# Attention over two buffers of exponentials, key scores inside the solve, diagonal blocks turned on chip

## The chip, the cores and the metric

One Trainium2 chip, of which the kernel uses one core. The metric is the device time of one execution in microseconds. Three runs of the kernel before took 1352.12, 1353.29 and 1354.02 us; the median is 1353.29.

## The reference

The kernel computes two layers: attention and a mixture of 64 experts, then a linear attention and a mixture of 8 experts, over two sequences of 512 tokens of width 256. Only the first attention is changed. Cut to what matters:

```python
# B = 2 sequences, T = 512, H = 16 heads of D = 16; q, k rotated (rope), scale = 1/4
s = einsum('bihd,bjhd->bhij', k, k) * scale        # keys against keys
e = exp(s - max over j < i), 0 where j >= i
p = e / sum(e)
A = eye(T) + p * beta[..., None]                   # unit lower triangular
u = solve_triangular(A, v, lower=True)
sc = einsum('bihd,bjhd->bhij', q, k) * scale, -inf where j > i
o = einsum('bhij,bhjd->bihd', softmax(sc), u)
x = x + o.reshape(B, T, 256) @ Wo
```

## The kernel before

The attention is worked in four units of eight heads of one sequence (UNITS = 4, GH = 8). In a unit the 512 rows are four blocks of 128 (NI = 4). The split bf16 parts of k and q lie in `stk`, three stacks (k, B, q) with two buffers each. TensorE, VectorE (dve), ScalarE (act), GpSimd (pool) and the DMA queue of SyncE (sp) each run one program written out by hand; semaphores order them. A unit passes these stages:

1. Row maxima. `row_scores` (L310) multiplies one head's scores into a bank pair `slot` of the PSUM tensor `scores`, and `maxima` (L571) reduces it on VectorE, one head and kind (key, query) at a time, sixteen rounds in all. `maxima` splits the eight heads' results in three bf16 parts, `turn_maxima` (L302) turns them, `rows` (L758) copies them to `mrow`, and SyncE puts them in the stacks as three more rows.
2. Key exponentials. `transposed_scores` (L323) gives one head's transposed scores less the maxima, `exps` (L764) its exponential in `E`, `select` (L847) on GpSimd clears the part above the diagonal. The sums over them are matmuls into `misc` (L355); their copy (L776), turn (L362) and `scale` (L592) give the factor `ng`, and turned again `G`.
3. Inversion. SyncE writes the diagonal blocks of `E` to DRAM (`edd`, L894) and reads their 32x32 blocks back turned, one per partition row, into `LB` (L900). `invert` (L615) multiplies by G (L624), runs 31 steps of products and sums (L638, L647) on VectorE, and copies the result turned (L651). SyncE writes both forms to DRAM (`xsd`) and reads them back into `XT` and `XR` (L910), which GpSimd has cleared.
4. Levels. In eight steps q the 32x32 inverses are joined to 64x64 (q below 4) and to 128x128: `sums` (L367) on TensorE, `scaled_sums` (L671) on VectorE, `join` (L387) on TensorE, `joined` (L654) on VectorE. Between the steps lie rounds of row maxima of the next unit: `maxima_due` (L244) gives which, all sixteen in unit 0 and the eight query ones in units 1 and 2.
5. Solve. `solve` (L411) with `solved` (L683): four steps, each a chain of matmul, bank copy on ScalarE (L809, L814), turn, and VectorE work, ending in a block of `U` (L697). In its last two steps four heads of the next unit's key scores are put in.
6. The next unit's key softmax (stage 2, the rest), then this unit's query exponentials, `attend` (L446) against U, `turn_outputs` and `outputs` (L701). The query exponentials lie in `EQ`, four heads deep, so that head 4 waits for the first half of `attend`.
7. For units 2 and 3, the eight key maxima ahead of the levels (`ahead`, L240), two slots at once.

VectorE's order in the loop over units is the spine of it:

```python
for q in range(8):
    if q: joined(u, q - 1)
    scaled_sums(u, q)
    for m in maxima_due(u + 1, q): maxima(u + 1, m, 0)
joined(u, 7); solved(u)
scale(u + 1); invert(u + 1)
outputs(u)
for m in range(ahead(u + 2)): maxima(u + 2, m, m % 2)
```

Ahead of the loop come the layer norm, the projections (`project`, L276) with rotation and split (`rotate_and_split`, L548), and stages 1 to 3 of unit 0.

## Time and profile before

| | |
|---|---|
| median of three runs | 1353.29 us |
| the profiled execution | 1339.94 us |
| its span | 1337.9 us |
| TensorE busy in the span | 823.5 us (62%) |
| VectorE | 569.6 us (43%) |
| ScalarE | 219.4 us (16%) |
| GpSimd | 250.8 us (19%) |
| granted TensorE clock, mean | 0.70 |

The profile is of one execution. Its span is 2.0 us shorter than that execution's own time. An instruction belongs to a line of the kernel; matmuls are pipelined and their ends are modelled. A clock of 1.00 is 2.4 GHz, one of 0.50 is 1.2 GHz.

### The profile page before, as it was taken

The page shows a single profiled execution, that of the slowest core. Times are in us where ns is not written, and L with a number is a line of the kernel's source. Part 1 is how long each engine was busy: PE and PEld are TensorE (multiplying, and loading weights), DVE is VectorE, ACT ScalarE, POOL GpSimd, SP SyncE. Part 2 cuts the span into 40 slices and gives each one's busy share as a digit, 9 for nine tenths or more (in the row PEclk, how much of TensorE's full clock was granted, in tenths as well). Part 3 has the DMA queues.
Part 4 walks back from the last instruction along what each step waited for, and adds up shares of the span by engine and source line. Part 5 has one row for each costly group of instructions (what it writes and reads, how often), then busy time and mean ns, then how long its engine had stood idle before and what let it go on. Part 6 is the DMA issues. An engine that isn't in the chain of part 4 may idle for free. (4 is left out here: it accounts for less than half of the span.)

```text
span 1337.9 us, 16296 instructions
## 1 busy us (share of the span) xinstructions
PE 823.5 (62%) x5790; PEld 538.4 (40%) x5791; DVE 569.6 (43%) x1712; ACT 219.4 (16%) x345; POOL 250.8 (19%) x303
## 2 busy tenths in 40 slices
PE   5376367675876687536740039999950455099990
PEld 3232145323632463134340028888840224056660
DVE  5265965158606850832154003333333655123332
ACT  1021000330033003300310013333310121021110
POOL 4010000230032003400106740000027710400004
PEclk9658655675567557655755569999975666599995
DMA  3605830088017602180049248887833300211113
GB/s 122 83 2 119 148 140 0 4 126 208 2 36 108 193 3 63 35 257 1 0 149 405 106 147 269 271 269 270 272 110 98 97 25 0 74 37 47 43 35 102
DMA packets 133774, 149.81 MB, mean 112 GB/s; under 512 B 57552, under 2 KB 96848, under 8 KB 132688
## 3 DMA queue, kind: packets, MB, share of 16 engines
q1 hardware_dynamic: 106032, 85.00, 22.8%
q10 hardware_dynamic: 20000, 43.00, 11.4%
q0 software_dynamic: 7680, 20.98, 4.9%
q8 instruction: 39, 0.64, 0.2%
q14 instruction: 23, 0.19, 0.0%
HBM read 81.89 MB, written 66.85 MB: 111 GB/s over the span
## 5 line engine op out<-in xcount | busy, mean ns | idle before, releaser
L576 DVE TENSOR_REDUCE nm<-scores 128x1 f32<-128x128 f32 (+3 forms) x256 | 106.3, 483 | 45.5 <-PE scores L319 45.0
L1023 PE MATMUL scores<-xgT,wgu 128*96 128x256 f32 x512 | 121.6, 380 | 0.0
L1092 DVE TENSOR_TENSOR hT<-sg,scores 96x256 f32<-96x256 f32 x64 | 26.7, 417 | 194.1 <-ACT sg L1129 194.1
L1213 POOL DMA_INDIRECT gb<-expert_outputs,gather_slots x64 | 66.9, 1045 | 223.6 <-SPq L1206 204.4
L854 POOL TENSOR_SCALAR_AFFINE_SELECT E<-E 128x256 f32<-128x256 f32 x64 | 24.5, 406 | 430.0 <-ACT E L769 430.0
L1000 PE MATMUL misc<-cf,xg 128*128 128x128 f32 x256 | 39.3, 277 | 93.6 <-DMA xg<-expert_rows 93.6
L1023 PEld LDWEIGHTS scores<-xgT,wgu 128*96 128x96 f32 x512 | 80.4, 164 | 20.8 <-issue 0.3
L1452 PE MATMUL scores<-w,xgT 128*128 x184 | 87.9, 601 | 0.3 <-issue 0.3
L316 PE MATMUL scores<-stack_B,stack_k 96*128 96x128 bf16 (+3 forms) x128 | 49.9, 468 | 53.1 <-DVE nm L576 25.0
L319 PE MATMUL scores<-cb 128*128 128x128 bf16 x256 | 80.0, 314 | 0.0
L1140 POOL DMA_INDIRECT expert_rows<-xn_moe,scatter_slots x64 | 62.5, 977 | 70.0 <-DVE gather_slots L1069 50.8
L1000 PEld LDWEIGHTS misc<-cf,xg 128*128 128x128 f32 x256 | 32.7, 143 | 100.1 <-issue 93.7
L1008 PE MATMUL scores<-wd,hT 96*128 96x256 f32 x256 | 65.9, 379 | 0.1
L1121 ACT COPY xgT<-misc 128x512 f32<-128x512 f32 x64 | 37.5, 586 | 158.5 <-PE misc L1000 158.5
L316 PE MATMUL scores<-stack_B,stack_q 96*128 96x128 bf16 (+3 forms) x128 | 50.2, 467 | 14.1 <-DVE nm L576 14.1
L638 DVE TENSOR_TENSOR tmp<-Y,LB 128x120 f32<-128x120 f32 (+35 forms) x244 | 53.4, 261 | 0.3
L647 DVE TENSOR_TENSOR Y<-Y,tmp 128x120 f32<-128x120 f32 (+35 forms) x244 | 53.4, 261 | 0.1
L762 ACT COPY mrow<-misc 96x128 bf16<-96x128 bf16 x8 | 2.1, 262 | 311.0 <-PE misc L306 311.0
L146 PE MATMUL misc<-cf,xn_lin 128*128 128x128 f32 x16 | 3.9, 426 | 79.9 <-DVE xn_lin L129 79.9
L1008 PEld LDWEIGHTS scores<-wd,hT 96*128 96x128 f32 x256 | 48.4, 190 | 8.9 <-DVE hT L1092 0.5
L1271 DVE SCALAR_TENSOR_TENSOR X<-gb,w,X 128x256 f32<-128x256 f32 x64 | 31.1, 485 | 43.9 <-DMA gb<-expert_outputs,gather_slots 42.3
L282 PE MATMUL scores<-xnT,early 128*128 128x512 f32 x64 | 32.2, 665 | 25.3 <-DVEq L556 24.7
(217 smaller groups left out, 1517.7 us busy)
## 6 DMA issues: line engine op xcount, KB each, us to landing
expert_rows<-zero ACTq DMA_DIRECT2D x32, 512.0 KB, 5.6
xg<-expert_rows SPq DMA_DIRECT2D x64, 256.0 KB, 4.3
expert_outputs<-yb SPq DMA_DIRECT2D x64, 256.0 KB, 3.9
wgu<-in_wgu SPq DMA_DIRECT2D x32, 384.0 KB, 3.3
diagonals<-E SPq DMA_DIRECT2D x16, 512.0 KB, 5.8
w<-in_w ACTq DMA_DIRECT2D x8, 1024.0 KB, 16.4
wd<-in_wd SPq DMA_DIRECT2D x32, 192.0 KB, 3.6
w<-in_w ACTq DMA_DIRECT2D x8, 512.0 KB, 19.1
```

Of the source, the lines that this page charges most:

```text
L316: nc.tensor.matmul(scores[:, slot, o:o + w], stk[c][0:KR, u % 2, h, it * P:w], stk["B"][0:KR, u % 2, h, 0:w], start=True, stop=False)
L319: ins = nc.tensor.matmul(scores[:, slot, o + w - P:o + w], identb, mask[c, it], start=False, stop=True)
L576: ins = nc.vector.tensor_reduce(nm[:, c, NI * h + it:NI * h + it + 1], scores[:, slot, o:o + (it + 1) * P], AX.X, ALU.max, negate=True)
L638: nc.vector.tensor_tensor(part, Yc[:, x, 0:n, k:k + 1].to_broadcast([P, n, w]), LB[:, k:k + 1, k + 1:SB].to_broadcast([P, n, w]), ALU.mult ...
L647: nc.vector.tensor_tensor(below, below, part, ALU.add).then_inc(s_inv, 1)
L1000: ins = nc.tensor.transpose(misc[:, j % 2, c:c + P], xg[:, j, t, k * P:(k + 1) * P], identf)
L1008: ins = nc.tensor.matmul(scores[:, j % 2, 512 + t * D:512 + (t + 1) * D], hT[:, j % 2, t * P:(t + 1) * P], wd[:, j // GE, j % GE, :], star ...
L1023: ins = nc.tensor.matmul(scores[0:F0, j % 2, g * CAP:(g + 1) * CAP], wgu[:, j // GE, j % GE, k, g * F0:(g + 1) * F0], xgT[:, j % 2, k, :], ...
L1121: nc.scalar.copy(xgT[:, j % 2].rearrange("p k n -> p (k n)"), misc[:, j % 2, :]).then_inc(s_xt0, 1)
L1140: pool.indirect_dma_start(out=xbuf, out_offset=bass.IndirectOffsetOnAxis(ap=isc[:, t, k:k + 1], axis=0), in_=xn[:, t, :], in_offset=None, ...
L1213: pool.indirect_dma_start(out=gb[:, g % NG, :], out_offset=None, in_=ybuf, in_offset=bass.IndirectOffsetOnAxis(ap=ig[:, t, k:k + 1], axis= ...
L1452: ins = nc.tensor.matmul(scores[:, j, g * F1:(g + 1) * F1], xgT[:, j, k, :], w13[:, bass.ds(e, 1), k, g * F1:(g + 1) * F1].rearrange("p e ...
```

## The change

- `E` has two buffers, `Eu(u)` for unit u, and both key and query exponentials of a unit lie in its buffer; early data (weights, ropes, parts, T1, U, XR) are put into space that is free at their time.
- All eight key scores of the next unit are put in the solve, one at each bank copy (two at the first). VectorE makes those bank copies.
- All sixteen row maxima of the next unit are in the levels of this one; a round reduces with one instruction to maxima of 128-column blocks (`bm`), and four small ones per kind finish them.
- The diagonal blocks are gathered by copies (ScalarE two quarters, VectorE two) and turned by VectorE; the inverses are turned by VectorE, `LB` and `turned` are read directly by the first level, and ScalarE fills `XT` and GpSimd `XR`. The DRAM tensors `edd` and `xsd` are gone.
- `joined` is on ScalarE, with T1 in two buffers by step.
- The denominators go to `scores` instead of `misc`; one query score stands before their turn. The first half of `attend` comes after head 5 instead of 4.
- Units run batch by batch: unit u is head group u % 2 of sequence u // 2.
- At the start the projections alternate with unit 0's key scores.
- Stores of parts, loads of stacks and the clearing of the expert rows move from ScalarE's queue to SyncE's; Wo and x are loaded (again) late.

```diff
-early = sba("early", [P, 4608])
+EE = sba("E", [P, 2, GH, WIDE])
+early = EE[:, 1].rearrange("p h n -> p (h n)")
 wqk = early[:, 0:2048].rearrange("p (a k d) -> p a k d", a=4, k=KT)
-T1 = early[:, 0:1024].rearrange("p (a h n) -> p a h n", a=2, h=GH)
-E = sba("E", [P, GH, WIDE])
+turned = sba("turned", [P, SB, SB])
+XR = X[:].rearrange("p t d -> p (t d)").rearrange("p (e c) -> p e c", c=64)
+T1 = shared[:, 0:1024].rearrange("p (a h n) -> p a h n", a=2, h=GH)
+U = shared[:, 1024:2048].rearrange("p (i h d) -> p i h d", i=NI, h=GH)
...
                     continue
                 for lo, hi in PAIRS:
-                    ins = nc.tensor.matmul(scores[hi, 1, 32 * h:32 * h + 32], e[lo, hi], XR[lo, x, 0:32],
...
                                            XT[64:128, x, 64:128], start=True, stop=True)
                     continue
                 for lo, hi in PAIRS:
                     if lo.start == 0:
-                        nc.tensor.matmul(scores[hi, 1, 512 + 32 * h:544 + 32 * h], XT[hi, x, hi],
...
+                    if not last:
+                        key_scores(u + 1, [2 * it])
                     pe.wait_ge(s_sn, 3 * u + it)
...
-                if u + 1 < UNITS and it >= NI - 2:
-                    key_scores(u + 1, range(2 * (it - NI + 2), 2 * (it - NI + 2) + 2))
+                if not last:
+                    key_scores(u + 1, [2 * it + 1] if it else [0, 1])
...
-        key_softmax(0)
-        pe.wait_ge(s_fa, 8)
-        for w in range(2, 8):
-            project(w)
-        pe.wait_ge(s_rf, 8)
+        pe.wait_ge(s_mr, 2)
+        project(2)
+        key_scores(0, [0, 1])
+        project(3)
+        key_scores(0, [2, 3, 4])
+        project(4)
+        key_scores(0, [5, 6, 7])
+        project(5)
+        project(6)
+        denominators(0)
+        project(7)
+        turn_denominators(0)
+        turn_g(0)
...
-            pe.wait_ge(s_xr, 16 * 3 * (u + 1))
-            pe.wait_ge(s_fa, 16 * u + 8)
+            pe.wait_ge(s_y, 2 * (u + 1))
+            if u:
+                pe.wait_ge(s_fa, use(1, u - 1) + GH)
+            else:
+                pe.wait_ge(s_rf, 8)
+                if q == 4:
+                    pe.wait_ge(s_xt, 4 * (u + 1))
+                    pe.wait_ge(s_xr, 2 * (u + 1))
                 sums(u, q)
                 if q:
                     join(u, q - 1)
                 if not last:
                     if q == 1:
-                        stacks_loaded(u + 1, "kq")
-                    for m in maxima_due(u + 1, q):
+                        stacks_loaded(u + 1)
+                    for m in maxima_due(q):
                         pe.wait_ge(s_fd, 16 * (u + 1) + m)
                         row_scores(u + 1, m, 0)
+                    if q == 5:
+                        turn_maxima(u + 1, 0)
             join(u, 7)
             if not last:
-                turn_maxima(u + 1, 0)
                 turn_maxima(u + 1, 1)
...
             solve(u)
             if not last:
-                key_softmax(u + 1)
+                denominators(u + 1)
+            pe.wait_ge(s_ml[1], 48 * (u + 1))
+            transposed_scores(u, 1, 0)
+            if not last:
+            for h in range(1, GH):
...
-                o = ROWAT[it]
-                ins = nc.vector.tensor_reduce(nm[:, c, NI * h + it:NI * h + it + 1],
-                                              scores[:, slot, o:o + (it + 1) * P],
-                                              AX.X, ALU.max, negate=True)
-            ins.then_inc(s_fd, 1)
+            nc.vector.tensor_reduce(bm[:, c, h, :],
+                                    scores[:, slot, 0:WIDE].rearrange("p (a n) -> p a n", n=P),
+                                    AX.X, ALU.max).then_inc(s_fd, 1)
...
+        def gather_blocks(u):
+            dve.wait_ge(s_dk, GH * (u + 1))
+            if u:
+                dve.wait_ge(s_y, 2 * u)
+            for s in range(2, P // SB):
+                for it in range(NI):
+                    to, of = diagonal_block(u, s, it)
+                    nc.vector.tensor_copy(to, of).then_inc(s_ga, 1)
+            dve.wait_ge(s_ga, 16 * (u + 1))
+            if u:
+                dve.wait_ge(s_xr, 2 * u)
+            link(nc.vector.transpose(LB[:].rearrange("p j i -> p i j"), Y[:]))
+            link(nc.vector.memset(Y[:], 0.0))
+            nc.vector.memset(flat[:, 0:SB * SB - 1].rearrange("p (a b) -> p a b", b=SB + 1)[:, :, 0], 1.0)
+            link(nc.vector.memset(flat[:, SB * SB - 1:SB * SB], 1.0))
...
+            if u:
+                dve.wait_ge(s_xt, 4 * u)
+            nc.vector.transpose(LB[:].rearrange("p c e -> p (c e)"), flat).then_inc(s_y, 1)
+            nc.vector.transpose(turned[:], Y[:].rearrange("p c i -> p i c")).then_inc(s_y, 1)
...
                 if it:
+                    dve.wait_ge(s_s, 3 * u + it)
+                    nc.vector.tensor_copy(bankT[:, 0:256], misc[:, 0, 0:256]).then_inc(s_sn, 1)
                     dve.wait_ge(s_st1, 3 * u + it)
                     link(nc.vector.tensor_tensor(
                         r, misc[:, 0, 0:2 * P].rearrange("p (h d) -> p h d", d=32)[:, :, 0:HD], g_, ALU.mult))
                     nc.vector.tensor_tensor(r, r, v, ALU.add).then_inc(s_r, 1)
                 else:
                     nc.vector.tensor_copy(r, v).then_inc(s_r, 1)
+                dve.wait_ge(s_us, 4 * u + it + 1)
...
         for m in range(16):
             maxima(0, m, m % 2)
+        for w in range(2, 6):
+            rotate_and_split(w)
+        gather_blocks(0)
+        rotate_and_split(6)
+        rotate_and_split(7)
         scale(0)
-        for w in range(2, 4):
-            rotate_and_split(w)
+        link(nc.vector.memset(U[:], 0.0))
+        link(nc.vector.memset(U[:, :, :, HD:HD + 1], 1.0))
         invert(0)
-        for w in range(4, 8):
-            rotate_and_split(w)
         for u in range(UNITS):
             last = u + 1 == UNITS
-            dve.wait_ge(s_xt, 16 * 4 * (u + 1))
-            dve.wait_ge(s_xr, 16 * 3 * (u + 1))
             for q in range(8):
-                if q:
-                    joined(u, q - 1)
                 scaled_sums(u, q)
                 if not last:
-                    for m in maxima_due(u + 1, q):
+                    for m in maxima_due(q):
                         maxima(u + 1, m, 0)
-            joined(u, 7)
             solved(u)
             if not last:
+                gather_blocks(u + 1)
                 scale(u + 1)
                 invert(u + 1)
             outputs(u)
-            if u + 2 < UNITS:
-                for m in range(ahead(u + 2)):
-                    maxima(u + 2, m, m % 2)
+        dve.wait_ge(s_x, 32)
...
-            if c and h == 4:
-                act.wait_ge(s_o, 2 * u + 1)
-            nc.scalar.activation(EQ(h) if c else E[:, h, :], scores[:, k % 2, 0:WIDE], ACT.Exp,
+            nc.scalar.activation(Eu(u)[:, h, :], scores[:, k % 2, 0:WIDE], ACT.Exp,
                                  scale=SCALE).then_inc(s_fa, 1)
...
         def key_softmax(u):
-            for h in range(2 if u else 0, GH):
+            for h in range(GH):
                 exps(u, 0, h)
+            act.wait_ge(s_dk, GH * (u + 1))
+            if u:
+                act.wait_ge(s_y, 2 * u)
+            for s in range(2):
+                for it in range(NI):
+                    to, of = diagonal_block(u, s, it)
+                    nc.scalar.copy(to, of).then_inc(s_ga, 1)
             act.wait_ge(s_den, u + 1)
-            nc.scalar.copy(bankT[:], misc[:, 0, :]).then_inc(s_dc, 1)
+            nc.scalar.copy(bankD[:], scores[:, 1, 0:512]).then_inc(s_dc, 1)
+        def fill_XT(u, s):
+            rows = slice(SB * s, SB * (s + 1))
+            nc.scalar.copy(XT[rows, :, rows], turned[rows].rearrange("p i e -> p e i")).then_inc(s_xt, 1)
...
-        for w in range(2, 8):
-            store_parts(act, w)
-            if w == 3:
-                load_stacks(act, 1)
         for u in range(UNITS):
-            for z in range(NZ // UNITS):
-                if z == 0:
-                    act.wait_ge(s_ones, 2)
-                    act.wait_ge(s_xt, 16 * 4 * (u + 1))
-                act.dma_start(xb_z[u * (NZ // UNITS) + z], zero[:]).then_inc(s_zf, 16)
+            act.wait_ge(s_y, 2 * (u + 1))
+            if u:
+                act.wait_ge(s_us, 4 * u)
+            fill_XT(u, 0)
+            fill_XT(u, 1)
+            joined(u, 0)
+            fill_XT(u, 2)
+            joined(u, 1)
+            fill_XT(u, 3)
+            for q in range(2, 8):
+                joined(u, q)
+                if q == 4 and u + 1 < UNITS:
+                    rows(u + 1, 0)
             if u + 1 < UNITS:
-                rows(u + 1, 0)
                 rows(u + 1, 1)
...
+        def fill_XR(u):
+            pool.wait_ge(s_y, 2 * u + 1)
+            for s in range(2):
+                rows = slice(SB * s, SB * (s + 1))
+                nc.gpsimd.tensor_copy(XR[rows, :, rows], LB[rows].rearrange("p c e -> p e c")).then_inc(s_xr, 1)
+                pool.wait_ge(s_xr, 2 * u + s + 1)
         select(0, 0)
+        pool.wait_ge(s_dk, GH)
         for u in range(UNITS):
+            fill_XR(u)
             if u + 1 < UNITS:
                 select(u + 1, 0)
-                pool.wait_ge(s_dk, GH * (u + 2))
-                pool.wait_ge(s_us, 4 * (u + 1))
-                link(nc.gpsimd.memset(XT[:], 0.0))
-                nc.gpsimd.sem_inc(s_z, 1)
-                link(nc.gpsimd.memset(XR[:], 0.0))
-                nc.gpsimd.sem_inc(s_z2, 1)
             select(u, 1)
...
-            sp.wait_ge(s_dk, GH * (u + 1))
-            for it in range(NI):
-                sp.dma_start(edd[u % 2].rearrange("(h i) j q -> i j h q", i=NI)[it],
...
-                    c = SB * (s % 2 if x else s)
-                    sp.dma_start(dst[SB * s:SB * (s + 1), :, c:c + SB],
-                                 xsd[u % 2, x, 32 * s:32 * s + 32]
-                                 .rearrange("e c i -> c e i")).then_inc(loaded, 16)
+        maxima_to_stack(0, 0)
+        maxima_to_stack(0, 1)
+        store_parts(sp, 2)
+        store_parts(sp, 3)
+        load_stacks(sp, 1)
+        for w in range(4, 8):
+            store_parts(sp, w)
+        sp.wait_ge(s_pw[0], 64)
+        sp.wait_ge(s_pw[1], 64)
+        for u in range(UNITS - 1):
+            maxima_to_stack(u + 1, 0)
+            maxima_to_stack(u + 1, 1)
+            if u + 2 < UNITS:
+                sp.wait_ge(s_fa, use(0, u) + GH)
+                load_stack(sp, u + 2, "k")
+            clear_rows(u)
+            if u + 2 < UNITS:
+                sp.wait_ge(s_fa, use(1, u) + GH)
+                load_stack(sp, u + 2, "B")
+                load_stack(sp, u + 2, "q")
+        clear_rows(UNITS - 1)
+        for z in range(NZ1):
+            n = min(4, TL - 4 * z)
+            sp.dma_start(xs[4 * z * P:(4 * z + n) * P, :].rearrange("(p n) d -> p (n d)", n=n),
+                         zero[:, 0:n * D]).then_inc(s_zf1, 16)
+        sp.wait_ge(s_o, 2 * (UNITS - 1))
+        sp.dma_start(wo0, a["wo0"].rearrange("(k p) n -> p k n", p=P)).then_inc(s_wol, 16)
+        sp.wait_ge(s_tt, 8 * UNITS)
```

## Rows read from the trace of the kernel before

**Rows 1.** Windows: length, busy us (instructions) by engine, granted clock, DMA share, GB/s.
```profile
170.00:237.00 67.00, 46.72 (x550) 32.84 (x554) 42.43 (x101) 0.52 (x2) 0.00 (x0) 0.50 0.18 70
...
326.00:367.00 41.00, 34.57 (x514) 26.80 (x514) 28.99 (x69) 0.52 (x2) 0.00 (x0) 0.50 0.18 70
...
672.00:1337.00 665.00, 398.00 (x1802) 288.07 (x1802) 230.91 (x621) 115.27 (x214) 161.32 (x160) 0.77 0.42 142
...
256.00:260.00 4.00, 2.50 (x28) 1.40 (x28) 0.88 (x3) 4.00 (x6) 1.53 (x4) 1.00 0.02 4
```

**Rows 2.** Timeline of VectorE: start, us, line, operation, count, idle before.
```profile
169.95 0.86 DVE L678 TENSOR_TENSOR early<-scores,ng 32x256 f32<-32x256 f32 x2 [0.25 <-DVE early L561]
...
259.47 0.29 DVE L697 COPY U<-misc 128x128 f32<-128x128 f32 x1 [2.16 <-PE misc L442]
...
286.37 1.23 DVE L624 TENSOR_TENSOR LB<-LB,G 128x1024 f32<-128x1024 f32 x1 [7.52 <-DMA LB<-diagonals]
...
309.71 1.03 DVE L651 COPY LB<-Y 128x1024 f32<-128x1024 f32 x1
...
327.25 0.86 DVE L678 TENSOR_TENSOR early<-scores,ng 32x256 f32<-32x256 f32 x2 [0.38 <-PE scores L382]
...
456.23 0.86 DVE L678 TENSOR_TENSOR early<-scores,ng 32x256 f32<-32x256 f32 x2 [0.38 <-PE scores L382]
...
579.83 0.86 DVE L678 TENSOR_TENSOR early<-scores,ng 32x256 f32<-32x256 f32 x2 [11.00 <-PE scores L382]
...
637.10 0.29 DVE L697 COPY U<-misc 128x128 f32<-128x128 f32 x1 [2.35 <-PE misc L442]
```

**Rows 3.** Timelines of TensorE and VectorE in the levels of unit 0.
```profile
204.80 1.65 PE L378 MATMUL scores<-XR,E 64*64 64x64 f32 x13
...
206.51 1.59 PE L398 MATMUL scores<-XT,early 64*64 64x64 f32 x13
...
172.67 0.42 DVE L664 COPY XR<-scores 32x256 f32<-32x256 f32 x1 [1.86 <-PE scores L406]
...
178.32 1.68 DVE L576 TENSOR_REDUCE nm<-scores 128x1 f32<-128x128 f32 x4 [1.77 <-PE scores L319]
```

**Rows 4.** Timeline of TensorE in the solves of units 0 and 3.
```profile
236.94 1.08 PE L434 MATMUL misc<-XT,R 128*32 128x128 f32 x16 [0.66 <-DVE R L695]
...
250.03 2.31 PE L330 MATMUL scores<-stack_k,stack_B 99*128 99x512 bf16 x8
252.14 0.64 PE L442 MATMUL misc<-cf,bankT 128*128 128x128 f32 x2
...
615.39 1.08 PE L434 MATMUL misc<-XT,R 128*32 128x128 f32 x16 [1.13 <-DVE R L695]
...
619.60 0.69 PE L427 MATMUL misc<-cf,bankT 128*128 128x128 f32 x2 [0.49 <-ACT bankT L809]
```

**Rows 5.** Timelines of TensorE and VectorE from the denominators to G, unit 1.
```profile
266.56 7.39 PE L355 MATMUL misc<-E,cf 128*32 128x512 f32 x64 [2.46 <-POOL E L854]
...
276.61 0.76 DVE L608 COPY G<-misc 32x32 f32<-32x32 f32 x4 [0.43 <-PE misc L365]
```

**Rows 6.** Groups by line and shape: count, busy us, mean ns of one, idle before.
```profile
L576 DVE TENSOR_REDUCE nm<-scores 128x1 f32<-128x512 f32 x64 | 43.6, 681 | 0.0
...
L576 DVE TENSOR_REDUCE nm<-scores 128x1 f32<-128x128 f32 x64 | 18.5, 289 | 45.5 <-PE scores L319 45.0
...
L769 ACT ACTIVATE E<-scores 128x1280 f32<-128x1280 f32 x32 | 37.2, 1246 | 3.8 <-PE scores L330 3.8
```

**Rows 7.** Timelines of TensorE and VectorE at the later projections.
```profile
113.46 13.95 PE L282 MATMUL scores<-xnT,early 128*128 128x512 f32 x32
...
117.15 0.69 DVE L553 TENSOR_TENSOR early<-scores,cf 128x512 f32<-128x512 f32 x1 [2.73 <-PE scores L282]
...
121.88 0.69 DVE L553 TENSOR_TENSOR early<-scores,cf 128x512 f32<-128x512 f32 x1 [0.22 <-DVE early L561]
```

**Rows 8.** DMA issues from 225 to 345 us: count, KB each, us to landing.
```profile
stack_q<-split_heads ACTq DMA_DIRECT2D x6, 128.0 KB, 7.2
```

296 lines of the change are left out of this document (129 added, 167 removed).

## The prediction

> **What bounds the kernel now.** I read the page first. Its chain that ended last starts at 1119 us and says nothing of the edited part, so I took the timelines of VectorE and TensorE, read off when each stage of the attention starts, and put the granted clock beside it from the windows. The attention ends near 672 us; the 665 us after it [rows 1] are not edited, and I leave them as they are. The attention is one serial loop over four units; VectorE's marks in it are [rows 2]: the first scaling of the levels, the last copy of U (end of the solve), the multiply that opens the inversion, the copy that closes it, and the next unit's first scaling. Unit 0 takes 327.25 - 169.95 = 157.3 us, unit 1 129.0, unit 2 123.6 [rows 2]. Unit 0 splits into levels 67.0 (to TensorE's first solve matmul at 236.94 [rows 4]), solve 22.8 (to 259.76), solve to inversion 26.6, inversion 23.3, inversion to the next levels 17.5 [rows 2]. In the last two kinds of gap VectorE mostly waits: for the denominators behind all eight exponentials, then for the diagonal blocks' trip through DRAM, then for the inverses' trip back. No engine is full; the order of the chain sets the time.
>
> **Levels, units 0 to 2.** The change puts all sixteen row-score rounds of the next unit here; before, unit 0 had sixteen, units 1 and 2 only eight. One round is a TensorE row score and a reduction, strictly in turn, for they share one bank. VectorE waits 1.77 us for the row score [rows 3]. Four reductions became one: the four sizes read 681 ns at 512 and 289 at 128 elements [rows 6], so 1.02 ns an element and some 158 ns fixed; one over 1280 is 1.49 us, against 1.68 for the four together [rows 3]. A round becomes 1.77 + 1.49 = 3.26 us. The joined copies leave VectorE, but TensorE still does sums and join between rounds: 1.86 us in the 32-wide level (the wait ahead of the first joined copy [rows 3]), and 204.80 to 208.10 = 3.3 us in the 64-wide one [rows 3]. So a round that follows sums and join takes 3.45 us (twice), 4.25 (at the change of level, an average of both) and 5.05 (three times). The first row score ends 4.3 us in (scaling 0.86, sums and join 1.7, score 1.7); nine plain rounds 29.3; the others 6.9 + 4.25 + 15.2; turning the key maxima 0.35; then the last reduction 1.6, four block reductions and four splits at about 0.22 each 1.75, the turn and its copy 1.3. Sum 64.9 us, where unit 0 had 67.0. Units 1 and 2 had some 40 us each (the window from 326 to 367 holds unit 1's [rows 1]), so there this part is a loss of 25 us each. The joined copies and the fills of XT on ScalarE (copies of 256 and of 1024 elements, 0.3 and 1 us by the 1246 ns of an exponential over 1280 [rows 6]) are hidden behind the rounds.
>
> **Solve.** Unit 3, with nothing put in, takes 615.39 to 637.39 = 22.0 us [rows 2, 4]. The change puts eight key scores there, each where TensorE waits for a bank copy. Unit 0 already has a pair in such a place: with it the next turn starts at 252.14, without it, by the plain hole of 0.49 us after the matmuls [rows 4], it would have started at 250.59, so a pair costs 1.55 us at the low clock. Two heads take 2.31 us [rows 4], 1.16 each, so a single one costs 0.4. Six singles and the first pair make 3.95, and seven copies on VectorE instead of ScalarE 0.05 each: 26.3 us. But behind the heads that the old kernel put in, the clock of 256 to 260 reads 1.00, 2.4 GHz, where the levels read 0.50, 1.2 GHz [rows 1]; with the clock up after the first two steps I get some 3.5 less, 22.8. I take 24.3, between the two, against 22.8.
>
> **Solve to inversion.** The exponentials are done but for the last: score, exponential 1.25 [rows 6], select and hand-over leave 1.4 us from the last U copy to the denominators. From their start to the end of G took 266.56 to 277.37 = 10.8 us [rows 5]; one query score now stands ahead of the turn, 0.3 more than the copy that it covers, and 0.15 to the multiply: 12.65 us instead of 26.6. The gathering (eight copies of 256 elements on VectorE and eight on ScalarE, some 3 us side by side, a turn, a fill of 0.9) lies under the 7.39 us of the denominators [rows 5] and has 3 us to spare; without this cover it would cost 6.5 a unit. No DRAM trip is left.
>
> **Inversion to levels.** The loop stays at 23.4. Two 32x32 turns of 1024 columns replace one copy of 1.03 us [rows 2]. No row shows a turn; below, it can't beat that copy of as many elements, above I allow twice it, so 2.1 to 4.2 for both. I take 2.2, since the copy is a reordering too. Then outputs 1.5, with the first sums beside them. So 3.8 us instead of 17.5: the round trip and the eight early maxima both go. The Trainium skill (VectorE: DVE Perf Modes, "The three transpose paths") gives 311 ns for a 128x128 bf16 turn; an estimate by columns is 2.5 us for 1024, and the whole sum would be 11 us longer by it, over four units.
>
> The cycle is 64.9 + 24.3 + 12.65 + 23.4 + 3.8 = 129.0 us. Against 157.3, 129.0 and 123.6 it gives -28.3, 0 and +5.4: **-22.9**. Units 1 and 2 gain some 25 us in the gaps and pay as much in the levels.
>
> **Unit 3.** No rounds; the levels took 579.83 to 615.39 = 35.6 us [rows 2, 4]. With the joined copies on ScalarE VectorE's scaling of one step lies beside the join of the last. The first four steps go by ScalarE (fill 1.0 and joined 0.9 a step), to 9.2 us, the last four by TensorE's 3.3 a step, to 23.2: -12.4. The solve pays 0.4. The first half of the attending is asked for one head later, which holds the last outputs by about one exponential [rows 6]: +1.5. Together **-10.5**.
>
> **Start.** The first sixteen maxima go from VectorE's pace (1.68 us and a hand-over) to that of TensorE's row scores, some 1.6 [rows 3]; two sets of block reductions take 1.7 back; about -1.7 in all. Then VectorE is the chain: six rotations at 4.73 (117.15 to 121.88 [rows 7]) of which four alternate with projections at some 5.9, gathering 6.5, scale 2.2, fill of U 1, inversion 23.4, turns 2.2. Projections are 3.5 us at the high clock (four in 13.95 [rows 7]). I get the first scaling at 160.8 instead of 169.95, and take **-8**. If the projections run at 1.2 GHz it is +7. SyncE now issues the parts' stores behind eighteen stack loads; the store that rotation 6 waits for is issued some 5 us in time.
>
> **Stack loads.** B and q of the unit after next start at the last query exponential. Six loads land in about 7.2 us [rows 8]; twelve take some 12, and the second step of the levels wants them 12 later. Between 0 and 4 us twice; I take **+2**. Clearing the expert rows moves to the same queue but is issued in the solve, when nothing else is wanted. POOL's fill of XR, XT's fill, wo0's and X's late loads have ten microseconds or more before they are asked for, and I cost them at nothing.
>
> **The sum** is -22.9 - 10.5 - 8 + 2 = -39.4 us. The profiled execution took 1339.94 us (2 us more than its span), so 1300.5; the median of the runs is 13.35 above it, and I carry that over: 1314 us.
>
> **A rule against the change.** The new inverses are read by TensorE with 128 bytes between elements, 40 small matmuls a step, 160 a unit, 640 in all. No row shows TensorE with such an operand; VectorE's closing copy reads so already, and takes 1.03 us for 1024 elements, one a cycle [rows 2]. The Trainium skill (SBUF - State Buffer, "Door 1: The DMA port swizzle") says that accesses which leave a 16-byte line pay a penalty; by the trace VectorE pays none.
>
> **Rivals.**
> 1. Strided operands slow TensorE (the side of slower). A small matmul is 42 ns now (40 in the 1.7 us of one step's sums and join [rows 3]). At a quarter of the rate each gains 126 ns, 81 us in all, 1395 us; from 62 ns each it eats the whole gain. VectorE's row speaks against: 5 in 100.
> 2. Key scores aren't hidden but lengthen the solve by their full 9.2 us: 6.5 a unit more than I count, 1334 us. The pair in unit 0 speaks against, 1.55 us for 2.31: 8.
> 3. The projections at the start find the low clock: 1329 us. Dense projections read 13.95 us for four after a dense stretch [rows 7], but here they are parted by key scores: 10.
> 4. The query part outlasts the inversion. I have it end 2.6 us before the turns do; POOL's selects or the later attending may cost 5 us more a unit and a stack load more: 1329 us: 10.
> 5. The levels find the high clock: row scores 0.85 instead of 1.67, 0.82 x 48 = 39 us less, 1275 us. TensorE was busy 34.6 of 41 us in unit 1's levels and stayed at 0.50 [rows 1]: 7.
> My forecast has 55, and 5 are left for what I don't see, mostly upward.
>
> **Numbers.** The range 1287 to 1340 takes in start (-14 to +7), solve (-5 to +6, both clocks), turns (0 to +8), loads (-2 to +6), and rivals 2, 3 and 4; it leaves out 1, 5 and the unseen, 17 in 100. What this kernel's measurement can tell from no change is about 0.2%, 2.7 us. Slower by more needs rival 1 or two unseen stalls: 6 in 100; within 3; faster 91.
>
> **What would show it.** Right: units 128 to 130 us apart in VectorE's first scalings; levels of 65 us in all of units 0 to 2 and 23 in unit 3; no wait on DMA ahead of the multiply; 12 to 13 us from the last U copy to it; levels within 4 us of the loop's end. Wrong: turns over 2 us each, small matmuls over 50 ns, a wait of TensorE on stack loads at the second step, a clock of 1.00 in the levels, or a query part that ends after the turns.

## The result and the profile after

The changed kernel takes 1297.9 us (median of 4 runs, 1293.08 to 1301.62) against 1352.7 before: a ratio of 0.959, 95% interval 0.956 to 0.963. I had forecast 1314 with a range of 1287 to 1340. The direction and the range held; the gain of 54.8 us is 39% larger than the 39.4 that I had summed up. The profiled execution took 1298.2 us (span 1296.3), and the attention ends 55.2 us earlier than in the old trace, at 605.8 instead of 661.0. So the whole gain lies in the edited part. In the second traces of both kernels, shown below, the attention ends at 610.2 and 660.8, which is 50.6 us. Times below are medians without the executions that ran slow: one of 1266.8 us of the kernel with the banks, and 1642.7 and 1788.7 of the kernel before.

VectorE's timeline of the changed kernel, with the marks that answer to [rows 2] and [rows 3]: start, us, line, operation, tiles, count, idle before.

```profile
123.83 0.69 DVE L567 TENSOR_TENSOR E<-misc,cf 128x512 f32<-128x512 f32 x1 [6.69 <-DMA split_heads<-E]
...
164.72 0.86 DVE L693 TENSOR_TENSOR xnT<-scores,ng 32x256 f32<-32x256 f32 x2 [1.24 <-PE scores L382]
...
172.45 1.49 DVE L588 TENSOR_REDUCE block_maxima<-scores 128x10 f32<-128x1280 f32 x1 [1.77 <-PE scores L320]
...
249.45 0.29 DVE L716 COPY xnT<-misc 128x128 f32<-128x128 f32 x1 [0.53 <-PE misc L444]
...
255.19 1.98 DVE L622 STREAM_TRANSPOSE LB<-Y 128x1024 f32<-128x1024 f32 x1 [1.83 <-ACT Y L794]
...
258.88 0.19 DVE L631 TENSOR_SCALAR den<-scores 128x32 f32<-128x32 f32 x1 [0.34 <-PE scores L359]
...
261.26 1.23 DVE L652 TENSOR_TENSOR LB<-LB,G 128x1024 f32<-128x1024 f32 x1
...
285.85 1.25 DVE L681 STREAM_TRANSPOSE LB<-Y 128x1024 f32<-128x1024 f32 x1
287.02 1.90 DVE L682 STREAM_TRANSPOSE turned<-Y 128x1024 f32<-128x1024 f32 x1
...
290.37 0.86 DVE L693 TENSOR_TENSOR xnT<-scores,ng 32x256 f32<-32x256 f32 x2
...
416.29 0.86 DVE L693 TENSOR_TENSOR xnT<-scores,ng 32x256 f32<-32x256 f32 x2
...
538.96 0.86 DVE L693 TENSOR_TENSOR xnT<-scores,ng 32x256 f32<-32x256 f32 x2
...
605.39 0.42 DVE L729 TENSOR_TENSOR AO<-misc,rec 128x256 f32<-128x256 f32 x1
```

What to see: the first scalings stand at 164.72, 290.37, 416.29 and 538.96, so the units take 125.7, 125.9 and 122.7 us where they took 157.3, 129.0 and 123.6 [rows 2]. The multiply has no wait on a transfer ahead of it any more (7.52 us before), and the next levels begin 4.5 us after the loop's end, not 17.5. Units 1 and 2 gain in the gaps too, but hand most of it back in the levels, where all sixteen rounds now stand, each of 1.77 us of waiting for TensorE and 1.49 of reduction, as summed. The first row is a surprise: rotation 6 waits 6.69 us for a store.

TensorE's timeline in the levels of unit 0, one 32-wide step, and under it, in a fence of its own, the same step of the kernel before. The strided operands of my first rival are in the first.

```profile
172.34 0.94 PE L382 MATMUL scores<-LB,E 32*32 32x32 f32 x26
...
174.01 0.25 PE L402 MATMUL scores<-xnT,turned 32*32 32x32 f32 x1
174.19 0.29 PE L317 MATMUL scores<-stack_B,stack_k 96*128 96x128 bf16 x1
```

```profile
178.21 0.91 PE L382 MATMUL scores<-XR,E 32*32 32x32 f32 x26
...
179.71 0.24 PE L406 MATMUL scores<-XT,early 32*32 32x32 f32 x2
180.06 0.29 PE L316 MATMUL scores<-stack_B,stack_k 96*128 96x128 bf16 x1
```

From the first of the 40 small matmuls to the next row score both take 1.85 us. The matmuls themselves are spread over 1.67 us (172.34 to 174.01) instead of 1.50, some 4 ns more each, and the row score follows them sooner. At the first step of unit 0 this is seen in the step too: 1.84 us instead of 1.68.

Windows of the changed kernel: levels of unit 0, the solves of units 0 and 2, and the end of unit 3; length, busy us and instructions by engine, granted clock, DMA share, GB/s. Under them, in a fence of its own, the end of unit 3 in the kernel before.

```profile
164.70:228.30 63.60, 46.96 (x546) 33.36 (x546) 32.60 (x45) 13.74 (x22) 1.01 (x1) 0.50 0.01 2
...
228.30:249.70 21.40, 17.82 (x206) 10.09 (x206) 5.84 (x17) 9.13 (x8) 5.36 (x14) 0.70 0.79 237
479.90:498.30 18.40, 14.72 (x206) 8.51 (x206) 5.89 (x17) 9.25 (x8) 5.35 (x14) 0.91 0.87 342
...
585.00:605.80 20.80, 13.61 (x103) 5.39 (x100) 1.35 (x4) 10.61 (x10) 6.11 (x16) 0.84 0.00 1
```

```profile
637.40:661.00 23.60, 16.99 (x104) 6.56 (x104) 1.36 (x4) 10.54 (x10) 6.12 (x16) 0.71 0.00 1
```

The same solve, instruction for instruction, takes 21.4 us at a mean clock of 0.70 and 18.4 at 0.91. The levels of unit 0 stay at 0.50, which is 1.2 GHz, as before; those of units 1 and 2 read 0.50 and 0.52.

The sum, term by term, in one profiled execution against the other:

| term | summed, us | read off, us |
|---|---|---|
| cycles of units 0 to 2 | -22.9 | -35.7 (-31.7, -3.1, -0.9) |
| unit 3 | -10.5 | -14.3 |
| start | -8 | -5.2 |
| stack loads | +2 | 0 |
| together | -39.4 | -55.2 |

and inside a cycle:

| part | summed | unit 0 | unit 2 |
|---|---|---|---|
| levels | 64.9 | 63.6 | 63.6 |
| solve | 24.3 | 21.4 | 18.4 |
| last copy of U to the multiply | 12.65 | 11.5 | 11.6 |
| inversion | 23.4 | 24.6 | 24.7 |
| to the next levels | 3.8 | 4.5 | 4.5 |

### The profile page after: what moved, and what is told of

Same layout as the page of the kernel before. It is cut to its first block and busy times, and to the rows that moved or that the text cites. A ratio compares the mean times of both kernels' runs of the same rounds, so it can differ in the third digit from the quotient of the medians.

```text
span 1296.3 us, 16178 instructions
## 1 busy us (share of the span) xinstructions
PE 798.2 (62%) x5790; PEld 529.6 (41%) x5791; DVE 571.6 (44%) x1556; ACT 284.9 (22%) x429; POOL 267.6 (21%) x305
## 5 line engine op out<-in xcount | busy, mean ns | idle before, releaser
L879 POOL TENSOR_SCALAR_AFFINE_SELECT E<-E 128x256 f32<-128x256 f32 x128 | 78.9, 641 | 419.5 <-ACT E L782 419.4
L588 DVE TENSOR_REDUCE block_maxima<-scores 128x10 f32<-128x1280 f32 x64 | 94.7, 1490 | 103.4 <-PE scores L320 103.3
L782 ACT ACTIVATE E<-scores 128x1280 f32<-128x1280 f32 x64 | 77.3, 1237 | 92.7 <-PE scores L331 92.3
L1041 PE MATMUL misc<-cf,xg 128*128 128x128 f32 x256 | 39.4, 277 | 93.5 <-DMA xg<-expert_rows 93.5
L1064 PEld LDWEIGHTS scores<-xgT,wgu 128*96 128x96 f32 x512 | 80.3, 164 | 20.8 <-issue 0.2
L1181 POOL DMA_INDIRECT expert_rows<-xn_moe,scatter_slots x64 | 62.5, 977 | 69.8 <-DVE gather_slots L1110 50.6
L320 PE MATMUL scores<-cb 128*128 128x128 bf16 x256 | 76.9, 303 | 0.0
L1162 ACT COPY xgT<-misc 128x512 f32<-128x512 f32 x64 | 37.5, 585 | 158.6 <-issue 101.7
L317 PE MATMUL scores<-stack_B,stack_q 96*128 96x128 bf16 (+3 forms) x128 | 47.1, 445 | 27.7 <-DVE block_maxima L588 27.6
L1661 POOL DMA_INDIRECT gb<-sorted_outputs,slots x16 | 16.2, 1015 | 149.6 <-DMA sorted_outputs<-yb 145.1
```

The lines of the kernel that those rows point to most:

```text
L317: nc.tensor.matmul(scores[:, slot, o:o + w], stk[c][0:KR, u % 2, h, it * P:w], stk["B"][0:KR, u % 2, h, 0:w], start=True, stop=False)
L320: ins = nc.tensor.matmul(scores[:, slot, o + w - P:o + w], identb, mask[c, it], start=False, stop=True)
L588: nc.vector.tensor_reduce(bm[:, c, h, :], scores[:, slot, 0:WIDE].rearrange("p (a n) -> p a n", n=P), AX.X, ALU.max).then_inc(s_fd, 1)
L782: nc.scalar.activation(Eu(u)[:, h, :], scores[:, k % 2, 0:WIDE], ACT.Exp, scale=SCALE).then_inc(s_fa, 1)
L879: ins = nc.gpsimd.affine_select(out=d, in_=d, pattern=[[0, 2], [1, P]], base=0, channel_multiplier=-1, compare_op=ALU.is_ge if c else ALU. ...
L1041: ins = nc.tensor.transpose(misc[:, j % 2, c:c + P], xg[:, j, t, k * P:(k + 1) * P], identf)
```

## The experiments

### The two kernels once more

> The changed kernel itself once more, beside the variants and with a second trace. Between the matmuls of the linear stage and the first relu the first trace of it has a hole of some 14 us on VectorE that the trace of the kernel before does not have. If that is a property of the changed kernel, it stands in this trace too, at the same place and of the same length. If it comes and goes from one execution to the next, it may be missing here or stand elsewhere. Theory: it comes and goes; the attention ends at 606 us, give or take 1, in either case. Time 1298, give or take 5.

Measured: 1299.8 us, ratio 0.960 (0.955 to 0.964). First scalings at 165.6, 291.4, 417.4 and 543.5, end of the attention at 610.2: the levels are 63.6 us in all three units again. I had expected the end at 606, give or take 1. Of the 4.4 us to the first trace 3.4 lie in unit 2's solve, 21.8 us in this trace and 18.4 in the first, and 0.9 in the start. The hole behind the linear stage is there as well (12.65 us on VectorE).

> The kernel before once more, for a second trace. Three traces of the changed kernel and its variants and the first one of this kernel differ behind the attention: relu of the linear stage starts some 27.4 us after the activations that turn xn there in the former and 8.7 us after in the latter. Theory: this time a kernel before has that hole as well, and the profiled execution that I predicted from, 13.35 us below the median, was the exception; then the attention ends at 661 us again and the rest takes some 690 us, the time is 1350 to 1355. Rival: the hole belongs to the changed program; then the trace shows relu after 8.7 us and the rest takes 677 us.

Measured: 1353.5 us, ratio 1.000 (0.998 to 1.002), and the attention ends at 660.8. ScalarE's timeline at the linear stage, first of the kernel before in this run, then of the same kernel in the execution that I predicted from:

```profile
1042.16 0.58 ACT L153 COPY xnT<-misc 128x512 f32<-128x512 f32 x1 [0.27 <-PE misc L146]
1070.27 1.26 ACT L1254 ACTIVATE relu<-scores,bias_lin 128x512 f32<-128x512 f32 x2 [27.52 <-remote]
```

```profile
1041.41 0.59 ACT L153 COPY xnT<-misc 128x512 f32<-128x512 f32 x1 [0.27 <-PE misc L146]
1050.07 1.27 ACT L1254 ACTIVATE relu<-scores,bias_lin 128x512 f32<-128x512 f32 x2 [8.07 <-PE scores L1230]
```

relu waits 27.5 us instead of 8.1 for something that the trace only calls remote. So the hole is no property of the change, and the 13.35 us between the profiled execution and the median, which I carried over without knowing them, are here: both kernels pay them. Of the fourteen traces here twelve show the wait, 27.1 to 28.4 us. The two without it are the one that I predicted from and that of the last experiment. That experiment ran on a chip where the kernel before has a median of 1338 us; beside all others it has 1353 to 1356. So the wait seems to go with the chip, which rests on one chip without it; on which one the first trace was taken is not known. What the engine waits for I can't say.

### Are the key scores hidden in the solve?

```
-                                if not last:
-                                    key_scores(u + 1, [2 * it])
...
-                            if not last:
-                                key_scores(u + 1, [2 * it + 1] if it else [0, 1])
...
                         if not last:
+                            key_scores(u + 1, range(GH))
                             denominators(u + 1)
```

> The eight key scores of the next unit leave the solve and stand in one row between it and the denominators. Theory, that they cost the solve next to nothing: the solve stays at 21 to 22 us (unit 3, with nothing put in, takes 21.0), the exponentials then go at their own pace of 1.25 us and a hand-over, eight of them 12 us, so the step from the last copy of U to the multiply grows from 11.5 to about 23, and the kernel by 11 x 3 = 34 us, to 1332. Rival, that they lengthen the solve by their full 1.16 us each: the solve falls by 9 us and the kernel grows by only 2 to 3 us a unit, to 1306. A second point: if the scores are what brings up the clock in the solve, the granted clock in the last 9 us of it falls from 0.99 to 0.50 here.

Measured: 1338.3 us, 38.5 above the changed kernel measured beside it. From the last copy of U to the multiply: 23.4, 22.5, 22.5 us. Windows of unit 0's solve in this kernel, its first 13.4 us and its last 9:

```profile
228.60:242.00 13.40, 8.99 (x104) 4.93 (x104) 3.45 (x10) 0.00 (x0) 0.00 (x0) 0.50 0.83 205
242.00:251.00 9.00, 6.26 (x75) 4.02 (x73) 2.43 (x7) 0.00 (x0) 0.00 (x0) 0.50 0.62 253
```

The solve without the scores takes 22.4, 21.5 and 21.4 us, with them 21.4, 21.7 and 18.4: eight scores of 1.16 us cost the solve nothing. Rival 2 of the prediction falls. In unit 0 they even pay for themselves: without them the clock stays at 0.50 to the solve's end, with them TensorE is busy 11.0 of the first 12.5 us and the clock of the next 8.9 us reads 0.99. It is no firm rule: in units 1 and 2 the last step took 6.5 us without them at a clock of 0.75, where unit 0's took 7.4 at 0.50.

### Who joins?

```
+                            if q:
+                                joined(u, q - 1)
                             scaled_sums(u, q)
```

(and the same function taken from ScalarE's list, where the four fills of XT then stand in a row)

> The joined copies go back from ScalarE to VectorE. Theory: in unit 3 they stand again in the chain with the scaling, and its levels grow from 25 us by about 8 (my prediction's -12.4 less what the fills cost there); in units 0 to 2 they lie partly beside the row score (copies 1.2 and scaling 0.86 against 1.67 us) and add 0.4 us a step, 3 us a unit. Together +17, 1315. Rival: the copies were hidden all along and the 10 us that unit 3's levels gained came from the inverses that no longer go through DRAM and from the clearing of the maxima: then unit 3 keeps its 25 us and the time stays within 3 us of 1298.

Measured: 1321.3 us, 21.5 above the changed kernel measured beside it. In the trace the levels of units 0 to 2 take 66.1 us (+2.5, expected 3), those of unit 3 take 36.3 instead of 24.3 (+12, expected 8). VectorE's timeline in unit 3, in this kernel and then in the changed one:

```profile
548.30 0.42 DVE L693 COPY X<-scores 32x256 f32<-32x256 f32 x1 [2.00 <-PE scores L405]
...
549.61 0.86 DVE L709 TENSOR_TENSOR xnT<-scores,ng 32x256 f32<-32x256 f32 x2
552.46 0.42 DVE L693 COPY X<-scores 32x256 f32<-32x256 f32 x1 [2.00 <-PE scores L405]
```

```profile
541.02 0.86 DVE L693 TENSOR_TENSOR xnT<-scores,ng 32x256 f32<-32x256 f32 x2 [1.21 <-PE scores L382]
543.09 0.86 DVE L693 TENSOR_TENSOR xnT<-scores,ng 32x256 f32<-32x256 f32 x2 [1.21 <-PE scores L382]
```

A step of 4.16 us becomes one of 2.07 with the copies on ScalarE. With them back on VectorE unit 3's levels are even longer than the 35.6 of the kernel before. So the whole of unit 3's 11.3 us (35.6 to 24.3) comes from where the joined copies are made, and none from the shorter way of the inverses.

### Is the round of 3.26 us what sets the levels?

```
-                        for it in range(NI):
+                        for n, (its, last_use) in enumerate(zip(BANKS, last_uses)):
+                          if last_use > 0:
+                            pe.wait_ge(s_fd, last_use)
+                          for it in its:
...
+                        for n in range(3):
+                            lo, hi = 4 * n, min(4 * n + 4, WIDE // P)
+                            dve.wait_ge(s_sa, 48 * u + 3 * m + n + 1)
-                        nc.vector.tensor_reduce(bm[:, c, h, :],
+                            nc.vector.tensor_reduce(bm[:, c, h, lo:hi],
```

> A round of row score and reduction is cut into its three banks: TensorE fills a bank as soon as the reduction of the last head has read that one. Theory, that the strict turns of 3.26 us set the levels of units 0 to 2: TensorE is busy 47 of the 63.6 us there and VectorE would be some 38, so the levels come down to TensorE's busy time and a little, about 50 us, -40 us in all and 1258. Rival 1, the denser TensorE gets its high clock in the levels: they go down to VectorE's 40 us, -70 us and 1228. Rival 2, the fixed cost of three reductions (0.3 us a round) and three hand-overs for one eats most of it: -10 us or less, above 1285.

Measured: 1253.0 us over three runs (1247.7 to 1259.2), ratio 0.926 (0.917 to 0.935), 46.8 below the changed kernel measured beside it. VectorE's timeline in unit 0's levels:

```profile
167.72 3.27 DVE L591 TENSOR_REDUCE block_maxima<-scores 128x4 f32<-128x512 f32 x6 [0.55 <-PE scores L324]
...
172.74 3.27 DVE L591 TENSOR_REDUCE block_maxima<-scores 128x4 f32<-128x512 f32 x6 [0.55 <-PE scores L324]
```

and the window of those levels:

```profile
164.20:210.30 46.10, 41.98 (x548) 28.96 (x547) 34.67 (x77) 13.81 (x22) 1.04 (x1) 0.61 0.01 2
```

A step with two rounds takes 5.02 us (167.72 to 172.74) where it took 6.71 (172.34 to 179.05 by TensorE's sums in the changed kernel), and VectorE waits 0.55 us in it for TensorE instead of 1.77 a round; the levels are 46.1, 45.6 and 47.8 us instead of 63.6, with TensorE busy for 42 of 46 in unit 0. I had expected some 50, so the theory holds and the gain is a little larger. The clock reads 0.61, 0.57 and 0.51 in the three, so for a part of the first two it was the high one (my rival 5, but in another kernel). The solves behind them took 18.4, 24.7 and 24.7 us and gave some of it back. The strict turn of score and reduction was the price of the levels, and TensorE's own work is the next.

### A trip through DRAM, put back

```
                         dve.wait_ge(s_inv, inverted[0])
+                        dve.wait_ge(s_yl, 16 * (u + 1))
...
+                    def trip(u):
+                        sp.wait_ge(s_inv, 122 * (u + 1))
+                        sp.dma_start(xsd, Y[:]).then_inc(s_ys, 16)
+                        sp.wait_ge(s_ys, 16 * (u + 1))
+                        sp.dma_start(Y[:], xsd).then_inc(s_yl, 16)
```

> Between the inversion and its two turns the inverses go to DRAM and back once, in plain rows of 4 KB (one store and one load of 512 KB; the kernel before had two stores and seven loads of single elements there). All computation stays. Theory, that what comes between inversion and levels is on the path: the trip of some 8 to 10 us is seen in full in each of the four units, +36 us, 1334. Rival (my fourth), that the query part ends later than the turns: then part of each trip is hidden, up to 5 us a unit, 1315.

Measured: 1335.5 us (three runs of 1334.6 to 1337.1 and one of 1319.0). VectorE's timeline behind unit 1's inversion:

```profile
299.16 1.25 DVE L684 STREAM_TRANSPOSE LB<-Y 128x1024 f32<-128x1024 f32 x1 [8.16 <-DMA Y<-inverses]
```

The four steps from multiply to turn are 6.3, 8.1, 9.1 and 6.4 us longer, the next scaling follows the turn as before (4.5 us behind it), and the attention ends at 642.0. Every trip is seen in full, so the way of the inverses is on the path of the changed kernel. In unit 0 of the kernel before it was not alone there: of its 17.5 us VectorE spent 13.7 on the eight early maxima (312.35 to 326.02), and TensorE's first sums waited for the last of these. In unit 2, which had none, the loop's end and the next scaling still lay 14.7 us apart (565.14 to 579.83), 11.00 of them waiting. What the loads of single elements added to a trip was not tried.

### One reduction or four

```
+                        for it in range(NI):
+                            o = ROWAT[it]
+                            ins = nc.vector.tensor_reduce(nm[:, c, h * NI + it:h * NI + it + 1],
+                                                          scores[:, slot, o:o + (it + 1) * P], AX.X, ALU.max, negate=True)
```

> Four reductions for each head's maxima instead of one, and no block maxima behind them. Theory: each round of the levels grows by 0.19 us (1.68 for 1.49) and each set saves a block reduction's 0.42: levels of units 0 to 2 grow from 63.6 to 65.8, three times, and the start by some 2 us, +9 in all, 1307. Rival: TensorE's share of a round hides part of it, the time stays within 3 us of 1298.

Measured: 1312.8 us. The levels take 65.1, 65.1 and 65.0 us, +1.5 each where I had 2.2, and the start 0.3 to 1.2 more. That is 5 to 6 us of the 13 that the time grew against the changed kernel. The rest is not in the rounds: in this trace unit 1's solve took 24.9 us and the step behind it 12.7, which is 4.3 more than in the changed kernel. The attention ends at 618.3, 8.1 us behind the second trace of the changed kernel, where I had expected 9 in all.

### The stores of the start

```
+                    for w in range(4, 8):
+                        store_parts(sp, w)
                     load_stacks(sp, 1)
-                    for w in range(4, 8):
-                        store_parts(sp, w)
```

> SyncE issues the stores of parts 4 to 7 ahead of the eighteen stack loads of unit 1. Theory: the 6.7 us that rotation 6 waits for a store at the start are the stores standing behind those loads; the wait goes, projection 7 takes part of it back, and the first scaling of the levels comes 4 to 6.5 us earlier (158 to 161 instead of 165), the kernel 4 to 6 us, 1293. The loads then start near 135 us and have landed before the second step of the levels wants them at about 166. Rival: the store itself is slow because the DMA engines are full, whatever its place: then the wait stays. Second rival: the loads come late now, and TensorE waits on DMA at the second step of the levels, 5 us or more: no gain.

SyncE's queue at the start: in the changed kernel, and then in this one. The last lines of each are from another view, the DMA issues from 100 to 126 us: count, KB each, us from issue to landing.

```profile
94.41 5.51 SPq L253 DMA_DIRECT2D split_heads<-E  x2
102.18 2.69 SPq L260 DMA_DIRECT2D stack_k<-split_heads  x6
...
107.75 2.80 SPq L260 DMA_DIRECT2D stack_q<-split_heads  x6
110.59 24.84 SPq L253 DMA_DIRECT2D split_heads<-E  x4
...
stack_q<-split_heads SPq DMA_DIRECT2D x6, 128.0 KB, 11.8
split_heads<-E SPq DMA_DIRECT2D x2, 384.0 KB, 13.2
```

```profile
92.51 34.43 SPq L253 DMA_DIRECT2D split_heads<-E  x6
127.04 2.97 SPq L260 DMA_DIRECT2D stack_k<-split_heads  x6
...
split_heads<-E SPq DMA_DIRECT2D x3, 384.0 KB, 2.5
```

In the changed kernel the store that rotation 6 waits for is issued at 110.59, and rotation 6 wants it at 117.1 (its start at 123.83 less the wait of 6.69). So it is issued 6.5 us in time. But it lands 13.2 us after its issue, where the same store lands in 2.5 us with the loads behind it: the data of the eighteen loads, 2.4 MB, are still on their way, the last six landing 11.8 us after their issue in the median. A landing in 2.5 us would have been early enough. Issuing the loads takes SyncE 8.4 us (102.18 to 110.55), which by itself would not have held rotation 6. That the landing and not the issue held it is worked out from these times; the run shows that the order of the two does.

With the stores first the wait is gone and the first scaling comes at 156.22, 8.5 to 9.4 us earlier. Of this 6.6 to 6.8 are the edit's, as expected: the way from the turn of the gathered blocks to the first scaling is 44.4 us instead of 51.0 and 51.2. The rest, 1.9 and 2.6 us, already stood at that turn, ahead of anything that the edit touches. But the kernel takes 1295.5 us, ratio 0.958 (0.955 to 0.960), which can't be told from 0.960 (its median is 4.3 us lower), and in its trace the attention ends at 605.7. Windows of unit 2's solve and of unit 3's end show where the gain went:

```profile
471.70:495.90 24.20, 20.63 (x206) 11.74 (x206) 5.85 (x17) 9.13 (x8) 5.35 (x14) 0.58 0.90 357
583.00:605.70 22.70, 16.73 (x104) 6.63 (x101) 1.37 (x4) 10.63 (x10) 6.12 (x16) 0.65 0.00 1
```

The same 206 matmuls take 24.2 us at 0.58 here, 21.4 at 0.70 and 18.4 at 0.91 in the changed kernel. The start's gain is real. In this execution units 2 and 3 took 4.8 us more than in the second trace of the changed kernel, with a lower clock in both places.

> The two edits that gained, together: rounds bank by bank and SyncE's stores ahead of the stack loads. The start gave 8.5 to 9.4 us in the trace of the one, the levels 17 us a unit in the other. Theory: both are on the chain and add up in it, first scaling near 156 us, levels 46 us; of the start's 9 us only some 3 came through to the time before, because the solves went to a lower clock, and that may come out either way: 1256 less 3 to 9, 1247 to 1253. Rival: with shorter levels the stack loads of unit 1 come late for the second step, TensorE waits on DMA there, and the gain of the start is lost: 1256.

Measured: 1247.0 us over six runs (1237.2 to 1254.8), ratio 0.921 (0.917 to 0.924): the best version, 6 us below the banks alone, though the two intervals overlap. The first scaling stands at 158.6, where I had expected 156, and TensorE waits on no stack load. Levels 46.1, 45.7 and 42.3 us. Windows of unit 2's levels and solve in it:

```profile
379.60:421.90 42.30, 37.05 (x550) 25.40 (x552) 34.38 (x77) 13.48 (x22) 0.72 (x1) 0.72 0.01 2
421.90:438.70 16.80, 13.11 (x206) 7.82 (x206) 5.89 (x17) 9.25 (x8) 5.36 (x14) 1.00 0.86 336
```

Here the high clock stood for nearly half of unit 2's levels (0.72 in the mean; 0.61 and 0.57 in units 0 and 1, as with the banks alone), and the solve behind them ran at 1.00: 16.8 us.

### The order of the units, and the attending

```
-                return u % 2, u // 2
+                return u // 2, u % 2
```

> The order of the units goes back to head group by head group, alone. I costed this part of the change at nothing. Theory: every transfer and every instruction has the same size in either order, the time stays within 4 us of 1298. Rival: the order matters for the stores and stack loads, the start or a cycle moves by 5 us or more.

Measured: 1296.4 us, ratio 0.956 (0.953 to 0.959), levels 63.6 us three times. The order makes no difference that these runs can tell.

```
-                            if h == 5:
+                            if h == 4:
                                 attend(u, 0)
-                            if h == 6:
+                            if h == 5:
                                 turn_outputs(u, 0)
```

(and the copy between them on ScalarE likewise)

> The first half of the attending, its copy and its turn go back one head earlier, as in the kernel before. Theory, my term of +1.5 us for unit 3: the attention's end comes 1.2 us earlier, and units 0 to 2 gain nothing, as there one select on GpSimd that is stuck for 8 to 10 us beside VectorE's inversion sets when the second half starts: 1297, not to be told from 1298. Rival: the query part is what the next levels wait for, then each unit gains some 1 us more, -5 in all, 1293.

Measured: 1303.3 us, ratio 0.963 (0.959 to 0.966): no gain. Its interval overlaps the changed kernel's, but it is 7 us above the run before, which was measured beside it, and the times of the two don't overlap (1294.8 to 1299.0 against 1300.0 to 1307.3). Where these microseconds come from stays open. The end of unit 3 takes 23.6 us in its trace, with a clock of 0.71, and 20.8 in the changed kernel's at 0.84. But in the eleven traces with the later attending that end takes anything from 20.7 to 23.6 us, so it says nothing on the order, for or against. The inversions, and the steps before and behind them, are the same. So my term of +1.5 is not to be seen, and the rival is out.

### A select that takes 8 us

The view of one line, GpSimd's selects in unit 0's query part of the changed kernel: count, shortest, median and longest duration in ns.

```profile
L879 POOL TENSOR_SCALAR_AFFINE_SELECT E<-E x14: 401/416/7916, 263.7 to 282.4; 128x256 f32<-128x256 f32 x14
its engine sat idle before it (us, times) until:
  ACT E L782: 9.5, 6
who waited for it (us, times):
  PEld misc L454: 7.5, 1
  PE misc L454: 7.1, 1
```

```
                             w = SB - 1 - k
+                            if u and k in (14, 20):
+                                dve.wait_ge(s_dq, GH * u - (k == 14))
```

> VectorE stops twice in the inversion of units 1 to 3, at its steps 14 and 20 of 31, until GpSimd has done the selects of the last unit's query heads up to the seventh and up to the eighth. Nothing else changes. In the trace of the changed kernel one of these selects takes 7.9 to 9.8 us in each unit where the others take 0.4, always in the middle of the inversion. Theory, that VectorE's uninterrupted row of small operations keeps GpSimd out: with the gaps no select takes more than 1 us, the second half of the attending starts some 4 us earlier in the unit (282.9 before), and the two stops cost VectorE 1 to 2.5 us a unit: 1298 plus 3 to 7 us. Rival, that the select is long for a reason of its own (or only in the record): it stays at 8 us or more and VectorE stands that long in each inversion, some 6 us a unit, 1316 or more.

Measured, on a chip where the kernel before takes 1338.0 us: 1288.7, ratio 0.963 (0.959 to 0.967); at the changed kernel's 0.960 it would be 1284, so +4 to 5, which the two intervals don't separate. The same view in this kernel, unit 0:

```profile
L881 POOL TENSOR_SCALAR_AFFINE_SELECT E<-E x11: 401/438/1778, 261.9 to 272.8; 128x256 f32<-128x256 f32 x11
```

and TensorE's second half of the attending in the same unit:

```profile
273.32 3.69 PE L454 MATMUL misc<-E,xnT 128*32 128x512 f32 x32 [2.33 <-POOL E L881]
```

The longest select falls from 7.9 to 1.8 us (to 1.7 and 2.9 in the next two units), where I had expected 1 or less; the second half of the attending starts 26.5 us behind the end of the last copy of U instead of 33.2, and the inversion grows by 0.3 to 0.9 us. VectorE's stream of small operations was what held GpSimd. The selects cost VectorE something too. At the start, with no select beside it, the way from the multiply to the turn takes 21.65 us in both kernels (138.79 to 160.44 in the changed one, 127.76 to 149.41 to the closing copy in the old). In the cycle of unit 0 it takes 24.6 with fourteen selects beside it and took 23.3 with eight: 0.21 us for each select, both times. That is read off, not tried.

## Why the prediction was right, and where its sizes were off

The forecast held by its range. The direction and the mechanism of each part are borne out by the experiments, but the sum was 15.8 us short of the trace. Some of that is chance: unit 2's solve at the high clock (3.4 us against the second trace) and the end of unit 3 (20.7 to 23.6 us over the traces).

**Start, -8 against -5.2.** The step that failed is the conclusion drawn from "the store that rotation 6 waits for is issued some 5 us in time". It was issued in time, by 6.5 us, but it landed 13.2 us after its issue, behind the data of the eighteen loads, and not after 2.5. I had looked at the issue and not at the landing. Against it, without the wait the first scaling stands at 156.2 and 158.6 in two traces, 2.2 to 4.6 us earlier than the 160.8 that I had worked out. 1.75 us of this is the inversion, which I took from the cycles at 23.4 us; at the start it takes 21.65, as the old trace already had it. The two errors partly cancelled.

**Levels, 64.9 against 63.6.** The round was right, and the experiment with the banks shows that it is what sets them. It is the same in all three units, as forecast.

**Solve, 24.3 against 21.4, 21.7 and 18.4.** This is the term that was mis-sized: 11.4 of the 12.8 us that the three cycles gained beyond my sum. I had taken the middle between 26.3 at the low clock and 22.8 with the clock up after two steps. Two of the three solves were the second case, and took 21.4 and 21.7. The third, 18.4, had the high clock after its first step, which I had not allowed for. Over all traces the solve with its eight scores has taken from 24.9 us (clock 0.56, up only in its last part) to 16.8 (1.00 throughout). So the saving of 3.5 for two steps fits, the base from which I took it was 1.1 to 1.4 us too high, the middle added 1.5, and the high bound was 6 us short. With the clock the short waits in the chain shrink too: VectorE's wait ahead of the copy of a product is 1.21 us in one step of unit 0 and 0.77 in the next, behind the rise.

**Solve to inversion, 12.65 against 11.5.** The denominators took 6.16 us at the higher clock, not 7.39. Gathering and its turn of 1.98 us lie beneath them with 0.34 us to spare ahead of the next scale, not 3: ScalarE's eight copies take 3.9 us, not the 3 that I gave both engines. The cover is nearly used up.

**Inversion, 23.4 against 24.6**, a loss of 1.2 that I did not have. "The loop stays at 23.4" left out that six more of GpSimd's selects now stand beside it, by the reading above 0.21 us each. **To the next levels, 3.8 against 4.5**: the two turns take 1.25 and 1.90 us, 3.1 with their overlap where I chose 2.2 between 2.1 and 4.2. The Trainium skill (VectorE: DVE Perf Modes, "The three transpose paths") has 311 ns for a 128x128 bf16 turn; by columns that is an estimate of 2.5 us for each, more than either took. The turn that reads from 128 bytes apart takes 0.65 us more than the one over plain rows (1.90 against 1.25).

**Unit 3, -10.5 against -14.3.** Levels -11.3 (summed -12.4), solve -0.3 (+0.4), the end -2.8 (+1.5). The last goes with its clock, 0.84 against 0.71, and not with the change: it was 23.6 again in another trace with the same order.

**Stack loads, +2 against 0.** No wait of TensorE on them in any unit.

**The rivals.** Strided operands: at most 0.17 us a step, some 4 ns for a small matmul where the rival had 126, 2.7 us over all sixteen steps, out. Whether the stride is what costs these was not tried. ("From 62 ns each" in the rival is 62 ns more each: the gain of 39.4 us over 640 matmuls.) Scores not hidden: out. Projections at the low clock: four of the six take 3.65 to 3.70 us, only the first and the last 5.2, and the first scaling without the stall is earlier than I had it, out. Query part: I had it end 2.6 us ahead of the turns, and it ends with them (second half turned from 288.10 to 289.21, the second turn of the inverses over at 288.92), for the one select that is held. It cost nothing, but the 2.6 us were not there. High clock in the levels: not in this kernel.
